# Moving the front of a kernel's second expert phase into the linear attention loop, with its results scattered by token into the output

## What is computed

```python
x = x + 0.5 * _L0_ffn_ref(_layernorm(x), ...)      # a local transformer, two layers
x = x + _L0_attn_ref(_layernorm(x), ...)
x = x + 0.5 * _L0_ffn_ref(_layernorm(x), ...)
x = x + 0.5 * _L1_ffn_ref(_layernorm(x), ...)      # mixture of experts, the first expert phase
x = x + _L1_attn_ref(_layernorm(x), ...)           # linear attention, the linear stream
x = x + 0.5 * _L1_ffn_ref(_layernorm(x), ...)      # the same experts again, the second expert phase
return x
```

```python
scores = jnp.einsum('bsh,he->bse', x, wr) + br
expert_id = jnp.argmax(scores, axis=-1)
h = jax.nn.gelu(jnp.einsum('bsh,ehf->ebsf', x, w1) + b1[:, None, None, :], approximate=False)   # 128 -> 512
y = jnp.einsum('ebsf,efh->ebsh', h, w2) + b2[:, None, None, :]                                  # 512 -> 128
out = jnp.einsum('ebsh,bse->bsh', y, jax.nn.one_hot(expert_id, E))
```

## Time and profile before

| what | us |
| --- | --- |
| median of 3 runs | 2564.29 (2558.7 to 2565.91) |
| the profiled execution's own time | 2567.91 |
| its span, first to last instruction | 2566.0 |
| TensorE busy | 2248.5 (88%) |
| VectorE busy | 1718.1 (67%) |
| ScalarE busy | 1463.6 (57%) |
| GpSimd busy | 1089.2 (42%) |
| mean granted TensorE clock | 0.953 of full |
| bytes moved by DMA | 73.63 MB |

### The profile page before, as it was taken

One profiled execution on the slowest core, in us unless ns is written; L12 is line 12 of the kernel. 1 busy time (PEld: TensorE's weight loads), 2 busy tenths in 40 slices (PEclk: granted clock), 3 DMA queues, 4 the chain that ended last, 5 costly groups with the idle time before them and its releaser, 6 DMA issues. The chain is left out here.

```text
span 2566.0 us, 52577 instructions
## 1 busy us (share of the span) xinstructions
PE 2248.5 (88%) x21574; PEld 1674.9 (65%) x21574; DVE 1718.1 (67%) x2800; ACT 1463.6 (57%) x2382; POOL 1089.2 (42%) x800
## 2 busy tenths in 40 slices
PE   2799999999999779999879999999999985878476
PEld 1577777777777556666547777777777753766276
DVE  3677777777788457777467777778878845533554
ACT  0467676666666425555547767676666643435342
POOL 4655556555565100000065655556556505410432
PEclk8899999999999879999879999999999987999898
DMA  7000000099999300000000000000000012210013
GB/s 148 1 1 1 2 2 2 1 94 114 107 102 117 25 1 2 2 2 2 1 1 2 2 1 2 1 2 1 2 2 2 1 52 64 57 51 1 32 53 96
DMA packets 185425, 73.63 MB, mean 29 GB/s; under 512 B 79658, under 2 KB 181204, under 8 KB 185060
## 3 DMA queue, kind: packets, MB, share of 16 engines
q1 hardware_dynamic: 177172, 56.68, 19.0%
...
## 5 line engine op out<-in xcount | busy, mean ns | idle before, releaser
L467 POOL TENSOR_TENSOR work<-work,rot_tables 128x512 f32<-128x512 f32 x256 | 446.5, 1764 | 443.7 <-ACT work L566 443.7
L475 POOL TENSOR_TENSOR work<-work 128x1024 f32<-128x1024 f32 x128 | 305.1, 2383 | 13.0 <-DVE work L885 3.1
L885 DVE TENSOR_TENSOR work<-work,rot_tables 128x1024 f32<-128x1024 f32 x128 | 162.2, 1267 | 112.1 <-ACT work L566 112.1
L1042 DVE TENSOR_REDUCE small<-psum 128x4 f32<-128x1024 f32 x128 | 156.5, 1223 | 92.5 <-PE psum L1550 92.4
L1276 PE MATMUL psum<-qkv_w_hi,h_hi 128*128 128x512 f32 x384 | 182.6, 476 | 18.9 <-POOL h_lo L494 16.4
L1430 PE MATMUL psum<-centered,ffn_w 128*128 128x256 f32 x768 | 190.4, 399 | 6.1 <-DVE centered L946 2.9
L902 DVE TENSOR_TENSOR work<-work,small 128x1024 f32<-128x1024 f32 x128 | 159.5, 1248 | 51.2 <-ACT small L580 47.0
L677 ACT ACTIVATE work<-psum 128x1024 f32<-128x1024 f32 x128 | 131.2, 1025 | 102.3 <-PE psum L1557 102.3
L1368 PE MATMUL psum<-work 64*128 64x128 f32 (+1 forms) x2048 | 181.1, 307 | 0.0
L482 POOL TENSOR_TENSOR y_all<-centered,squared 64x256 f32<-64x256 f32 x64 | 48.5, 759 | 296.2 <-ACT squared L626 293.6
L1430 PEld LDWEIGHTS psum<-centered,ffn_w 128*128 128x128 f32 x768 | 145.8, 196 | 36.3 <-DVE centered L946 17.7
...
## 6 DMA issues: line engine op xcount, KB each, us to landing
...
```

The source lines that it names most:

```text
L467: last = pool.tensor_tensor(b[:, :, :, o_], a[:, :, :, i_], tab[:, l, 1, t, :, o_].unsqueeze(2).to_broadcast([P, 2, HEADS, 32]), ALU.mult)
L475: pool.tensor_tensor(rC[:, t, :], rC[:, t, :], rB[:, t, :], ALU.add).then_inc(f_sum, 1)
L885: dve.tensor_tensor(g(rC[:, t, :]), g(rA[:, t, :]), tab[:, l, 0, t, :, :].unsqueeze(2).to_broadcast([P, 2, HEADS, DH]), ALU.mult)\
L1042: dve.tensor_reduce(dst, PS[:, 0:2, :].rearrange("p b (t j) -> p b t j", t=TILES), AX, ALU.max, negate=True).then_inc(a_smax, 1)
```

## The change

1. *Front.* The pieces of the front become functions of their own (`m_mean_`, `m_center`, ...). For n = 0 they run as before. For n = 1 they are called inside `lin`'s steps: pair j begins (`m_mean_`, `m_center`) in step 7 + 2j, when both its sequences have their attention added, and ends (`m_position`) in step 11 + 2j. `lin` gets four more steps for it.
2. *Banks.* The second front uses bank 7 for mean and variance, 6 for rows, 1 for scores and ranks. `lin` takes bank 0 for both mean and variance and bank 4 for both kv and projection, with new waits: `var(s)` for `center(s + 1)`, `masked(s)` for `proj(s - 2)`, `mean(s)` for `rstd(s - 2)`, `kv(s)` for `x_out(s - 3)`.
3. *Router.* The matmul with 136 columns is split in both phases into one with the 8 router columns and a transpose, in different banks; scores and rows are read without waiting for each other.
4. *Residual.* In the second phase TensorE also transposes `X` for the pair (`m_x_rows`), ScalarE copies it into `hrow` (`m_x_out`), and a row of `h_area` has 257 floats: features, token number, residual. Nine more DMAs fill those columns beforehand.
5. *Results.* In the second phase `y_out` writes result plus bias into `ysum`, and a second instruction writes 0.5 times that plus the tile's residual; GpSimd scatters this by token number into the output, with a bounds check that drops rows with a number beyond 4095. The second back and the final transposes, copies and stores are gone.
6. *Slots.* `xtile` has 8 slots in place of 6, in both phases. The gelu's tiles lie in memory of the first transformer (`sqs`).

The core of the diff:

```diff
+HX = HW + D
...
+XT = 8
...
-        xtile = [sb(f"tile_x{n}", [P, HW]) for n in range(6)]
+        xtile = [sb(f"tile_x{n}", [P, HX]) for n in range(XT)]
...
+        def rows_done(i):
...
+            return i + 1 if i < PAIRS else PAIRS + 2 * (i - PAIRS + 1)
...
+        def front_banks(i):
...
+            return (0, 1, 4 + i % 2, 2 + i % 2) if i < PAIRS else (7, 7, 6, 1)
...
+                    if n == 1:
+                        sp.dma_start(area[:, :, HW:HX], ones[:, :].unsqueeze(1).to_broadcast([P, m, D])).then_inc(blank, 16)
...
-                    if i >= 6:
-                        sp.wait_ge(m_yout[(i - 6) % 4], 16 * ((i - 6) // 4 + 1))
+                    if i >= XT:
+                        sp.wait_ge(m_yout[(i - XT) % 4], 16 * ((i - XT) // 4 + 1))
                     r = sp.value_load(rows[0:1, j:j + 1], min_val=0, max_val=SLOTS - P)
-                    sp.dma_start(xtile[i % 6][:, :], h_area[n][bass.ds(r, P), :]).then_inc(m_xin[i % 6], 16)
+                    sp.dma_start(xtile[i % XT][:, 0:(HW, HX)[n]], h_area[n][bass.ds(r, P), :]).then_inc(m_xin[i % XT], 16)
...
+                if n == 0:
+                    y_t = y_tokens[0:AREA, :].rearrange("(t p) d -> p t d", p=P)
+                    for q in range(BACK):
+                        m = TT // BACK
+                        sp.dma_start(yin[:, q * m:(q + 1) * m, :], y_t[:, q * m:(q + 1) * m, :]).then_inc(m_back[q], 16)
...
-            out_t = io["out"].rearrange("b (n p) d -> p (b n) d", p=P)
-            for q in range(8):
-                sp.wait_ge(xT_sb, q + 9)
-                sp.dma_start(out_t[:, 4 * q:4 * q + 4, :], xin[:, 4 * q:4 * q + 4, :]).then_inc(stored, 16)
-            sp.wait_ge(stored, 16 * 8)
...
-                    pool.wait_ge(m_rows, i + 1)
+                    pool.wait_ge(m_rows, rows_done(i))
...
-                        pool.indirect_dma_start(out=h_area[n], in_=hrow[i % 3][:, t, :], in_offset=None,
+                        pool.indirect_dma_start(out=h_area[n], in_=hrow[i % 3][:, t, 0:(HW, HX)[n]], in_offset=None,
...
+                    off = bass.IndirectOffsetOnAxis(ap=to, axis=0)
+                    if n == 0:
+                        pool.indirect_dma_start(out=y_tokens, out_offset=off, in_=yrow[i % 4][:, :], in_offset=None)\
+                            .then_inc(m_yout[i % 4], 16)
+                    else:
+                        pool.indirect_dma_start(out=out_rows, out_offset=off, in_=yrow[i % 4][:, :], in_offset=None,
+                                                bounds_check=AREA - 1, oob_is_err=False).then_inc(m_yout[i % 4], 16)
...
+            def m_rows_out(i):
+                act.wait_ge(m_routed, i + 1)
+                free(act, m_scat[i % 3], 64 * (i // 3))
+                act.activation(hrow[i % 3][:, :, 0:D], PS[:, front_banks(i)[2], :].rearrange("p (t d) -> p t d", t=4),
+                               ACT.Copy).then_inc(m_rows, 1)
+
+            def m_x_out(i):
+                act.wait_ge(m_xrow, i - PAIRS + 1)
+                act.activation(hrow[i % 3][:, :, HW:HX], PS[:, front_banks(i)[2], :].rearrange("p (t d) -> p t d", t=4),
+                               ACT.Copy).then_inc(m_rows, 1)
...
+                for k in range(SEQS + 10):
+                    if k % 2 == 1 and 0 <= k - 11 < SEQS:
+                        m_x_out(PAIRS + (k - 11) // 2)
+                    if k % 2 == 0 and 0 <= k - 8 < SEQS:
+                        m_square(PAIRS + (k - 8) // 2)
+                    if k % 2 == 1 and 0 <= k - 9 < SEQS:
+                        m_root(PAIRS + (k - 9) // 2)
+                    if k % 2 == 0 and 0 <= k - 10 < SEQS:
+                        m_rows_out(PAIRS + (k - 10) // 2)
...
+                        dve.wait_ge(m_y, i - 1)
+                        link(dve.tensor_tensor(ysum[i % 2][:, :], PS[:, 4 + i % 2, 0:P], wbuf[i % 5][:, B2:EW], ALU.add))
+                        dve.scalar_tensor_tensor(out=yrow[i % 4][:, :], in0=ysum[i % 2][:, :], scalar=0.5,
+                                                 in1=xtile[i % XT][:, HW:HX], op0=ALU.mult, op1=ALU.add).then_inc(m_y, 1)
...
-                    dve.tensor_tensor(lcen[s % 3], X[:, s, :], PS[:, 7 * (s % 2), 0:T], ALU.subtract).then_inc(l_cen, 1)
+                    dve.tensor_tensor(lcen[s % 3], X[:, s, :], PS[:, 0, 0:T], ALU.subtract).then_inc(l_cen, 1)
...
+                    free(dve, l_proj, s - 1)
...
+                for k in range(SEQS + 10):
+                    if k % 2 == 0 and 0 <= k - 10 < SEQS:
+                        m_picked(PAIRS + (k - 10) // 2)
+                    if k % 2 == 1 and 0 <= k - 11 < SEQS:
+                        m_position(PAIRS + (k - 11) // 2)
                     if 0 <= k - 3 < SEQS:
                         masked(k - 3)
                     if 0 <= k - 5 < SEQS:
                         x_out(k - 5)
                     if k < SEQS:
                         center(k)
+                    if k % 2 == 1 and 0 <= k - 9 < SEQS:
+                        m_normed(PAIRS + (k - 9) // 2)
                     if 0 <= k - 4 < SEQS:
                         o_norm(k - 4)
                     if 0 <= k - 1 < SEQS:
                         normed(k - 1)
+                    if k % 2 == 1 and 0 <= k - 7 < SEQS:
+                        m_center(PAIRS + (k - 7) // 2)
...
-            for q in range(8):
-                dve.wait_ge(xT_ready, q + 9)
-                dve.tensor_copy(xin[:, 4 * q:4 * q + 4, :].rearrange("p n d -> p (n d)"), R[q // 4][:, q % 4, :])\
-                    .then_inc(xT_sb, 1)
...
+            def m_router(i):
+                _, _, b, c = front_banks(i)
+                ahead = 2 if i < PAIRS else 1
+                pe.wait_ge(m_h, i + 1)
+                free(pe, m_rows, rows_done(i - ahead) if i >= ahead else 0)
+                free(pe, m_base, i + 1 - ahead)
+                for t in range(4):
+                    h_ = mh[i % 3][:, t * P:(t + 1) * P]
+                    pe.matmul(PS[:, c, t * NE:(t + 1) * NE], h_, wr[:, :], start=True, stop=True)
+                    last = pe.transpose(PS[:, b, t * P:(t + 1) * P], h_, eye[:, :])
+                last.then_inc(m_routed, 1)
+
+            def m_x_rows(i):
+                pe.wait_ge(m_rows, rows_done(i) - 1)
+                for t in range(4):
+                    last = pe.transpose(PS[:, front_banks(i)[2], t * P:(t + 1) * P],
+                                        X[:, 2 * (i % PAIRS) + t // 2, (t % 2) * P:(t % 2 + 1) * P], eye[:, :])
+                last.then_inc(m_xrow, 1)
...
-                    free(pe, l_cen, s - 1)
-                    pe.matmul(PS[:, 7 * (s % 2), 0:T], ones[:, :], X[:, s, :], start=True, stop=True).then_inc(l_mean, 1)
+                    free(pe, l_cen, s)
+                    free(pe, l_rstd, s - 1)
+                    pe.matmul(PS[:, 0, 0:T], ones[:, :], X[:, s, :], start=True, stop=True).then_inc(l_mean, 1)
 
                 def var(s):
                     pe.wait_ge(l_sq, s + 1)
-                    free(pe, l_rstd, s)
-                    pe.matmul(PS[:, 1, 0:T], ones[:, :], sqr[s % 2][:, :], start=True, stop=True).then_inc(l_var, 1)
+                    pe.wait_ge(l_cen, min(s + 2, SEQS))
+                    pe.matmul(PS[:, 0, T:2 * T], ones[:, :], sqr[s % 2][:, :], start=True, stop=True).then_inc(l_var, 1)
...
+                    free(pe, x_done, SEQS * 4 + s - 2 if s > 2 else 0)
...
-                    pe.matmul(PS[:, 6, 0:T], lw[:, wp:wp + P], lout[s % 2], start=True, stop=True).then_inc(l_proj, 1)
+                    pe.matmul(PS[:, 4, T:2 * T], lw[:, wp:wp + P], lout[s % 2], start=True, stop=True).then_inc(l_proj, 1)
...
+                    if k % 2 == 1 and 0 <= k - 9 < SEQS:
+                        m_router(PAIRS + (k - 9) // 2)
+                    if k % 2 == 1 and 0 <= k - 7 < SEQS:
+                        m_mean_(PAIRS + (k - 7) // 2)
+                    if k % 2 == 0 and 0 <= k - 8 < SEQS:
+                        m_var_(PAIRS + (k - 8) // 2)
+                    if k % 2 == 0 and 0 <= k - 10 < SEQS:
+                        m_ranks(PAIRS + (k - 10) // 2)
+                        m_x_rows(PAIRS + (k - 10) // 2)
```

262 lines of the change are left out of this document (117 added, 145 removed).

## The result

The changed kernel takes **2493.68 us** (median of 4 runs, 2490.33 to 2498.76), the kernel before 2562.82 (4 runs): ratio 0.9739, 95% interval 0.9714 to 0.9763. The forecast was 2497, its range 2480 to 2526. The profiled span is 2492.4 us, 73.6 less than before; the working had 67.

The account below looks back on a forecast made before the run. No engine bound it; waits did, for tiles a 6.94 us loop carrying three. Terms -17 - 14 - 14 - 22 = -67 took the profiled 2567.9 to 2500.9; profile lying 3.6 above the median, forecast 2497 us, range 2480 to 2526.

Parts of the forecast that it names:

- Eight slots, first phase: First expert phase's tiles: step falls from 2.39 to TensorE's 1.95 us, -17 us.
- the loop: Tile phases: result DMA, load into freed slot, down matmuls; 6.94 us, three tiles before, five with eight slots, binding past 9.75.
- Second phase's tiles: Second expert phase: step falls from 2.44 to 2.08 us, VectorE slowest at 2.05, checked scatter costing 0; -14 us.
- SP's waits for results: Tile phases: SP's 32 waits for results to land, 51.4 us in all, would be gone.
- The front in the stream: Second expert phase's front inside the linear stream: a pair takes 14.6 us against 16.7, first load near 2426, -14 us.
- Step a: Linear steps: shared banks make masking wait for the projection and delay the variance, 0.5 us more a step.
- The end: After the last results land: read-back, transposes, residual and store vanish, nothing replaces them, -22 us.
- Edits at nothing: Second fill of the wide area and first front's router in 12 passes: cost taken as 0.
- Rival A: Interleaving front and linear stream does not pay because of unforeseen waits; merge gains 0, 2511 us; chance 0.20.
- C: Both tile phases: eight slots don't help since landings grow, steps stay at 2.3 us, 2519 us; chance 0.05.
- B: Second phase's tiles stay near 2.44 us or worse because VectorE binds, 2511 or 2531 us; chance 0.10.
- D: Second phase: the checked scatter, 2.5 us dearer or more, makes the kernel slower than before, 2580 us; chance 0.03.

Follow-up runs that it names:

- slots runs: Kernel before with eight tile slots instead of six, 2525.64 us; changed kernel with six instead of eight, 2551.14 us, and with seven, 2512.72 us.
- one result: Changed kernel with one VectorE instruction for the second phase's result, leaving out the expert's output bias: 2497.80 us.
- no copy: Changed kernel without VectorE's copy of the weights from tile 5 of the second phase on: 2501.91 us.
- busy waits: Changed kernel with ScalarE's and VectorE's even merged steps reordered, plus unread TensorE matmuls in waits around the linear stream's start: 2500.13 us.
- six slots unchecked: Changed kernel with six slots and second-phase results scattered without bounds check into an internal area, output not written: 2542.79 us.
- front apart: Changed kernel with the second expert phase's front run after the linear stream, which keeps its new banks: 2523.53 us.
- before, eight slots: Kernel before with eight tile slots instead of six, nothing else: 2525.64 us.
- unchecked: Changed kernel with second-phase results scattered without bounds check into an internal area, padding rows written, output not written: 2503.09 us.

## Why the prediction was right, term by term

- **Eight slots, first phase: -17, measured -19.1.** The mechanism is shown by the slots runs. I took 1.95 for TensorE's step with "the small gaps of other quiet steps"; those gaps came from the loop itself and went with it, 1.88.
- **Second phase's tiles: -14, measured -19.4.** The term rested on VectorE setting the pace at 2.05, 2.08 with losses. Its cycle did become the longest, but at 1.93, and in the 39 tiles it never held TensorE up: the transposes are 1.89 apart but for late loads, and relieving VectorE ("one result", "no copy") gained nothing. So the step had its engine wrong as well as its size. The size was off by one overlap: I took 0.08 off once, while transposed copy and result overlap by another 0.08 (2471.62 + 0.28 against 2471.82). The new instruction took 0.29, not 0.31, and its wait 0.03. Forecasting a cost of zero for wide loads and the check came out right only because of the slots, which is luck as much as judgement: the loop grew to 8.85 us, of the 9.75 that I gave as its limit, where I had added no more than 1.9 to 6.94. I had said that a scatter above 1.3 us would show me wrong: its median is 1.27, its longest 1.53.
- **SP's waits for results** are not gone, as I had said they would be: 30.8 us in 29 waits, against 51.4 in 32. They are waits for slots filled ahead of need.
- **The front in the stream: -14, measured -15.5** (ramp to first tile 165.6 against 181.1). Close by errors that cancel, so the good number is in part luck. Step a was right in kind, 0.40 a step for 0.5. The merged pair takes 13.64 for my 14.6: the router's twelve passes took 1.14 (2325.81 to 2326.95) for 1.6, and the even step's variance starts at 3.49 for 3.95. Steps 9 to 16 took 53.2 us for 58.4. On the other side stands the ramp with the first four steps, 5.6 us longer than before where seven steps at 0.40 give some 3; 2.2 of it went away with the busy waits, which kept the clock up. And the durations that I listed behind step 17 add up to 31.4 us, to 2413.4 and not to the 2416 that I wrote; no row stood for the rest. From the start of step 17 to the last positions it took 35.3.
- **The end: -22, measured -18.4.** The step that failed is "the program ends when they land". From the last transpose to the last scatter it takes 7.69 us, 0.85 more than before (6.84): 0.33 for the second instruction and 0.52 for the later start of the checked scatter, which I had taken at 0 as hidden; nothing hides it in the drain (7.35 in "one result", 7.23 with six slots unchecked). And from the last scatter's start to the end it is 5.15 us, where 2.31 passed before from the last scatter to the read-back (2541.59 to 2543.90): 2.84 more. The scatter lands after 2.2, and behind that almost 3 us follow in which no engine row and no transfer stands. The kernel before had less of such a close: its DMA engines moved output until 2565.2, 0.8 us before its end. Why it is longer here stays open.
- **Edits at nothing:** the first front, router and all, costs nothing that shows: from its first mean matmul to its phase's first load it is 63.2 us (2103.95 to 2167.1), 62.7 before (2105.56 to 2168.3). The fill moved 17 MB more and ended near 907 for my 930.

Rival A is refuted by "front apart", C by "before, eight slots". B named the engine with the longest cycle, but it held nothing up in the changed kernel; only in "unchecked" did it, at 2.00. D had the right suspect, the checked scatter, at a fifth of the price it needed (0.52 us for 2.5); with six slots the checked scatter into the output makes up 14.8 of the 19.4 us by which the second phase is slower than before (112.1 against 97.3, and 92.7).
